# A graph network's attention layer: its prologue cut into three spans of nodes

## The reference, cut to what matters

```python
h = jnp.maximum(_layernorm(x, axis=-1), 0.0)
x = x + _L3_gnn_ref(h, src, dst, L3_gnn_qTrans, L3_gnn_kTrans, L3_gnn_vTrans)
...
q = (rowEmb @ qTrans).reshape(-1, HEADS, head_dim)
k = (colEmb @ kTrans).reshape(-1, HEADS, head_dim)
v = (colEmb @ vTrans).reshape(-1, HEADS, head_dim)
att = jnp.clip(jnp.einsum('ehd,ehd->eh', q, k), -10.0, 10.0)
expAtt = jnp.exp(att)
attNorm = jax.ops.segment_sum(expAtt, rows, num_segments=n_nodes)[rows]
att = expAtt / (attNorm + 1e-08)
res = (att[:, :, None] * v).reshape(-1, EMB)
out = jax.ops.segment_sum(res, rows, num_segments=n_nodes)
```

## Time and profile before

| | us |
|---|---|
| median of 3 runs | 2742.87 (2740.80 to 2744.53) |
| the profiled execution | 2741.29 |
| its span, first to last instruction | 2739.6 |
| DVE busy in it | 1842.0 (67%) |
| POOL busy | 1266.8 (46%) |
| PE busy | 1204.0 (44%) |
| ACT busy | 783.7 (29%) |

### The profile page before, as it was taken

One profiled execution on the slowest core, in us unless ns is written; L12 is line 12 of the kernel. 1 busy time (PEld: TensorE's weight loads), 2 busy tenths in 40 slices (PEclk: granted clock), 3 DMA queues, 4 the chain that ended last, 5 costly groups with the idle time before them and its releaser, 6 DMA issues. The chain is left out here.

```text
span 2739.6 us, 40317 instructions
## 1 busy us (share of the span) xinstructions
PE 1204.0 (44%) x12203; PEld 596.2 (22%) x12203; DVE 1842.0 (67%) x3710; ACT 783.7 (29%) x1927; POOL 1266.8 (46%) x973
## 2 busy tenths in 40 slices
PE   1111111111111111111110169978799629998898
PEld 1111111111111111111110023333343413333334
DVE  9988788888888888888885101111201539999997
ACT  0000000133332223121111300000000229999996
POOL 2788888888888888888888000000000000100001
PEclk6555555555555555555555589999899859999997
DMA  6776776689888889775666998889579282333231
GB/s 222 240 220 191 222 221 182 141 216 222 202 218 217 206 210 221 161 156 125 135 148 130 283 421 355 350 361 416 217 286 366 76 132 84 88 88 88 85 87 48
DMA packets 506207, 550.60 MB, mean 201 GB/s; under 512 B 129536, under 2 KB 452669, under 8 KB 504381
## 3 DMA queue, kind: packets, MB, share of 16 engines
q1 hardware_dynamic: 137773, 303.52, 30.9%
q10 hardware_dynamic: 255792, 245.78, 27.9%
q0 software_dynamic: 112608, 0.85, 9.7%
HBM read 381.75 MB, written 168.31 MB: 201 GB/s over the span
## 5 line engine op out<-in xcount | busy, mean ns | idle before, releaser
L610 POOL DMA_INDIRECT table<-amount,cell x782 | 1210.6, 1548 | 295.8 <-issue 281.1
L431 DVE SCALAR_TENSOR_TENSOR equal<-key_row,keys,masks 128x1280 bf16<-128x1280 f32 (+9 forms) x790 | 692.2, 943 | 0.2 <-DVE parts L417 0.2
L563 PE MATMUL totals<-parts_g,equal 128*128 128x6 bf16 x4345 | 129.0, 167 | 1022.8 <-DVE is_tile L440 1022.6
L283 ACT ACTIVATE w_tile<-cells 128x128 f32<-128x128 f32 x600 | 179.2, 301 | 779.4 <-issue 769.3
L563 PEld LDWEIGHTS totals<-parts_g,equal 128*128 128x128 bf16 x4345 | 122.2, 104 | 1034.3 <-DVE is_tile L440 1034.0
L944 PE MATMUL banks<-tiles,xs_pair 128*64 128x512 f32 (+1 forms) x1512 | 316.5, 567 | 5.8 <-DMA tiles<-counts_dram 5.0
L1257 POOL MEMSET o_t<- 128x64 f32 x1 | 0.2, 151 | 650.6 <-POOLq L719 650.6
L1267 POOL COPY v_tile<-v_all 128x128 f32 x175 | 51.6, 296 | 506.1 <-PE banks_d L1320 432.8
L423 DVE SCALAR_TENSOR_TENSOR equal_tail<-key_row,keys,masks 128x1280 bf16<-128x1280 f32 x156 | 235.2, 1546 | 20.1 <-issue 17.1
L1305 PE MATMUL banks_d<-q,k 96*128 (+2 forms) x700 | 194.5, 368 | 80.3 <-DMA k<-parts_dram 47.1
L1152 ACT ACTIVATE att<-banks_d,shift 128x1024 f32<-128x1024 f32 (+1 forms) x175 | 199.2, 1138 | 76.4 <-PE banks_d L1305 76.0
(11 more groups left out here) (226 smaller groups left out, 1513.0 us busy)
## 6 DMA issues: line engine op xcount, KB each, us to landing
table<-zeros ACTq DMA_DIRECT2D x100, 800.0 KB
cells<-table ACTq DMA_DIRECT2D x24, 3200.0 KB
key_row<-keys_dram SPq DMA_DIRECT2D x79, 640.0 KB
tiles<-counts_dram SPq DMA_DIRECT2D x27, 1664.0 KB, 10.0
tiles<-weights_dram SPq DMA_DIRECT2D x27, 1664.0 KB, 9.5
tiles<-counts_dram SPq DMA_DIRECT2D x27, 1536.0 KB, 8.7
tiles<-weights_dram SPq DMA_DIRECT2D x27, 1536.0 KB, 8.3
weights_dram<-w_tile ACTq DMA_DIRECT2D x24, 1600.0 KB
```

The source lines that it names most:

```text
L283: ins = nc.scalar.activation(w_tile[:, b, s], cells[:, s, :, 0], ACT.Copy, accum_out=deg_parts[:, s, bass.ds(t, 1)])
L431: ins = nc.vector.scalar_tensor_tensor(equal[b][:, OWN_AT[j]:OWN_AT[j + 1]], key_row[:, b, j * P:GE], keys[:, bass.ds(g * G + j, 1)], own_ ...
L563: nc.tensor.matmul(sums, equal[b][:, at:at + P], parts_g[:, b, j, :], start=False, stop=True, skip_group_check=True)
L610: nc.gpsimd.indirect_dma_start(out=table, out_offset=bass.IndirectOffsetOnAxis(ap=cell[:, b, j:j + 1], axis=0), in_=amount[:, b, j, :], in ...
```

## The change

The prologue is cut in three spans of columns, `SPANS`: chunks 0 and 1 (1024 columns, 8 tiles), chunks 2 and 3 (1024), and chunks 4 to 6 (1152). PE mixes its transposes and projections chunk by chunk; ACT alone does all 14 copies; DVE splits span by span. `parts_dram` now has the layout of `q6` and `k6`: head, block, feature. SP stores for each span twelve pieces of 64 rows, one for each of the six blocks of q and of k, so a part that stands in three blocks is stored three times. It then reloads each span with two DMAs of 96 rows and 4 heads. PE waits for the first span before the first score; the other two waits stand at tiles 8 and 16 of the first chunk, whose steps are written out instead of looped.

```diff
-    parts_dram = nc.dram_tensor("parts_dram", [3, 2, HEADS, HD, NR], BF16, kind="Internal").ap()
+    parts_dram = nc.dram_tensor("parts_dram", [2, HEADS, NPART, HD, NR], BF16, kind="Internal").ap()
+    SPANS = [(0, 2), (2, 4), (4, len(CHUNKS))]
+    span_cols = [slice(CHUNKS[a][0], sum(CHUNKS[b - 1])) for a, b in SPANS]
...
-            keep(0)
-            keep(1)
-            place(0)
-            keep(2)
-            place(1)
-            place(2)
+            def keep(span):
+                for part_no in range(3):
+                    sp.wait_ge(parts_ready, 3 * span + part_no + 1)
+                    for side, part_of in ((0, QPART), (1, KPART)):
+                        for n in range(NPART):
+                            if part_of[n] == part_no:
+                                sp.dma_start(parts_dram[side, :, n, :, span_cols[span]],
+                                             part[side * D:(side + 1) * D, part_no, span_cols[span]]
+                                             ).then_inc(parts_stored[span], 16)
+
+            def place(span):
+                sp.wait_ge(parts_stored[span], 16 * 2 * NPART)
+                for side, to in ((0, q6), (1, k6)):
+                    sp.dma_start(to[:, :, span_cols[span]],
+                                 parts_dram[side, :, :, :, span_cols[span]].rearrange("h n d c -> (n d) h c")
+                                 ).then_inc(rows_placed[span], 16)
+
+            for span in range(3):
+                keep(span)
+                place(span)
             blocks = counts_dram.rearrange("(s p) d -> p s d", p=P)
...
+            copy_h(0)
+            for n in range(len(CHUNKS)):
+                if n + 1 < len(CHUNKS):
+                    copy_h(n + 1)
+                copy_qk(n)
...
-            for n in range(3):
-                nc.vector.tensor_copy(part[:, n], qk_t[:]).then_inc(parts_ready, 1)
-                dve.wait_ge(parts_ready, n + 1)
-                if n < 2:
-                    link(nc.vector.tensor_tensor(qk_t[:], qk_t[:], part[:, n], ALU.subtract))
+            for span, (_, last) in enumerate(SPANS):
+                dve.wait_ge(qk_copied, last)
+                rest = qk_t[:, span_cols[span]]
+                for n in range(3):
+                    piece = part[:, n, span_cols[span]]
+                    nc.vector.tensor_copy(piece, rest).then_inc(parts_ready, 1)
+                    dve.wait_ge(parts_ready, 3 * span + n + 1)
+                    if n < 2:
+                        link(nc.vector.tensor_tensor(rest, rest, piece, ALU.subtract))
...
+            turn_chunk(0)
+            turn_chunk(1)
             for n, (c0, w) in enumerate(CHUNKS):
-                pe.wait_ge(h_t_ready[n % 2], n // 2 + 1)
+                pe.wait_ge(h_t_ready, n + 1)
                 nc.tensor.matmul(banks[:, n, 0:w], k["qk"][:], h_t[:, c0:c0 + w], start=True, stop=True
                                  ).then_inc(qk_ready, 1)
-            for e in range(2):
-                pe.wait_ge(qk_copied[e], 1)
+                if n + 2 < len(CHUNKS):
+                    turn_chunk(n + 2)
+            pe.wait_ge(qk_copied, len(CHUNKS))
...
-            pe.wait_ge(rows_placed, 16 * 2 * NPART)
+            pe.wait_ge(rows_placed[0], 32)
...
+                    if first:
+                        for t in range(2, T):
+                            for span in (1, 2):
+                                if t * P == span_cols[span].start:
+                                    pe.wait_ge(rows_placed[span], 32)
+                            step(t, t % RING, t // RING)
+                        return
...
-            with pe.Fori(0, SC - 1) as ci:
+            chunk(0, 4, 4, first=True)
+            with pe.Fori(1, SC - 1) as ci:
                 chunk(ci, 4, 4)
```

More of the change, by code:

```diff
@@ L1042, in attention_layer @@
     h_ready, turned = sem("h_ready_d"), sem("turned_d")
-    h_t_ready, qk_copied = [sem(f"h_t_ready{e}") for e in range(2)], [sem(f"qk_copied{e}") for e in range(2)]
+    h_t_ready, qk_copied = sem("h_t_ready"), sem("qk_copied")
     qk_ready, parts_ready, v_cleared = sem("qk_ready"), sem("qk_parts_ready"), sem("v_cleared")
     parts_stored = [sem(f"parts_stored{n}") for n in range(3)]
-    rows_placed = sem("rows_placed")
+    rows_placed = [sem(f"rows_placed{n}") for n in range(3)]
     v_made, v_copied = sem("v_made"), sem("v_copied")
@@ L1068, in over_tiles @@
                 body(RING * i + j, j, c_reg * USES + i, c_reg * T + RING * i + j)
[L1070 to L1078, removed]
     N_SCORED = -(-N // 64) * 64
@@ L1139, in _, with copy_h, copy_qk @@
             nc.scalar.activation(stat[:, 2], stat[:, 1], ACT.Sqrt).then_inc(std_ready, 1)
-            copy_banks(act, nc.scalar.copy, 0)
+            def copy_h(n):
+                act.wait_ge(turned, n + 1)
+                c0, w = CHUNKS[n]
+                nc.scalar.copy(h_t[:, c0:c0 + w], banks[0:D, n, 0:w]).then_inc(h_t_ready, 1)
+            def copy_qk(n):
+                act.wait_ge(qk_ready, n + 1)
+                c0, w = CHUNKS[n]
+                nc.scalar.copy(qk_t[:, c0:c0 + w], banks[:, n, 0:w]).then_inc(qk_copied, 1)
+            copy_h(0)
[3 more added lines that the diff above has]
+                copy_qk(n)
             act.wait_ge(consts_set, 2)
@@ L1177, in _ @@
             nc.vector.memset(shift[:, 1:2], -CLIP).then_inc(consts_set, 1)
-            copy_banks(dve, nc.vector.tensor_copy, 1)
-            for e in range(2):
-                dve.wait_ge(qk_copied[e], 1)
-            for n in range(3):
-                nc.vector.tensor_copy(part[:, n], qk_t[:]).then_inc(parts_ready, 1)
-                dve.wait_ge(parts_ready, n + 1)
-                if n < 2:
-                    link(nc.vector.tensor_tensor(qk_t[:], qk_t[:], part[:, n], ALU.subtract))
+            for span, (_, last) in enumerate(SPANS):
[7 more added lines that the diff above has]
+                        link(nc.vector.tensor_tensor(rest, rest, piece, ALU.subtract))
             dve.wait_ge(v_made, 1)
@@ L1275, in _, with turn_chunk @@
             pe.wait_ge(h_ready, 1)
-            for c0, w in CHUNKS:
+            def turn_chunk(n):
+                c0, w = CHUNKS[n]
                 for t in range(c0 // P, (c0 + w) // P):
@@ L1291, in _, with steps @@
             pe.wait_ge(consts_set, 2)
-            pe.wait_ge(rows_placed, 16 * 2 * NPART)
+            pe.wait_ge(rows_placed[0], 32)
             pe.sem_inc(counts_turned, RING)
             pe.sem_inc(values_added, RING)
-            def steps(ci, width):
+            def steps(ci, width, first=False):
                 W = columns(width)
@@ L1345, in steps, with chunk @@
                 return scores_of, tiles, values_of
-            def chunk(ci, width, next_width):
-                scores_of, tiles, values_of = steps(ci, width)
+            def chunk(ci, width, next_width, first=False):
+                scores_of, tiles, values_of = steps(ci, width, first)
                 tiles()
```

## The result

| | us |
|---|---|
| before, median of 6 | 2742.59 |
| changed kernel, median of 6 | 2759.48 (2755.57 to 2766.86) |
| ratio | 1.0066, 95% interval 1.0053 to 1.0079 |
| forecast | 2784 (2747 to 2808), slower 0.78 |

The direction was right and the time is in the range, but the slowdown is 17 us where 42 were forecast. The rival "four engines that don't meet" (2753) came nearer.

What follows compares the result with a forecast made beforehand. It took the loop's start, held by stores, reloads and the first counts, to shift the end, ACT and DVE being full. Counts at 2283.2 against 2240.98 gave +42: 2783.5, stated as 2784 us, range 2747 to 2808.

Steps and rivals of the forecast that it cites:

- four engines that don't meet: Rival on the prologue's stores: 1.26 and 1.42 us each, +11 us, 2753; chance 0.27.
- first span stored: Prologue, span 0: 2.5 us fixed plus twelve stores at 2.1 us after the first part, stored at 2205.3.
- The order: SP's queue: first load of counts comes behind `place(2)`, so the loop still starts behind all three spans.
- Four engines: Prologue stores: destination's outermost size 4 gives each store four DMA engines at most; share 0.25.
- sixteen: Rival on the stores: rows dealt over 16 engines, 0.3 us a store, 21 us earlier, 2722; chance 0.16.
- The price of one store: 64-row store on four partly meeting engines: 2.1 us (2.36 for 1152 columns), between 1.26 free and 2.5 halved.
- The lower bound: Best price of a 64-row store: four engines at 26 GB/s each, 104 GB/s together, 1.26 us.
- The full price for four engines: Port rule, engines 0 and 2, 1 and 3 meeting in every store: stores 94 us instead of 79, end 15 us later.
- The first part: Prologue's first split: first part ready at 2177.6 instead of 2184.60, 7 us gained; a 512-column projection costed at 0.90 us.
- The reload: Two 96-row reloads per span at 300 GB/s: 5.2 us, 5.9 for the third span.
- the fixed part: Time from a DMA's issue to its landing beyond the transfer itself, taken as 2.5 us.
- The cover: Prologue: split, ACT's 14 copies (8 us) and PE's v matmuls (8.03 us) stay hidden if stores take longer than DVE.

Runs made afterwards that it cites:

- e3: Changed kernel with SP's queue reordered: first loads of counts issued between the spans instead of behind the third reload; 2742.13 us, 0.9990 of before.
- e8: e1 with loads of counts between the spans as in e3, dealt out otherwise (tiles 0-4, 5-6, 7-12); 2705.11 us, 0.9862 of before.
- e1: Changed kernel with the 64 rows ordered feature, head, so a store's destination is one block and sixteen engines store; 2727.74 us, 0.9949 of before.
- e2: Changed kernel with every store read from partitions 32 to 95, so no two of four engines read 32 apart (traffic only); 2758.99 us, 1.0052 of before.
- e7: Changed kernel with one span of 3200 columns instead of three, and rows ordered feature, head for sixteen engines; 2742.41 us, 1.0000 of before.

## Why the prediction was wrong in size

By its own steps, against the profile after. Each duration runs from one event to the next, on SP's queue except for the first and the last (PE's transposes).

| step | forecast | measured | difference |
|---|---|---|---|
| first transpose to first part | 5.9 | 8.3 | +2.4 |
| first span stored | 27.7 | 21.3 | -6.4 |
| reload and second span | 32.9 | 23.4 | -9.5 |
| reload and third span | 36.0 | 25.8 | -10.2 |
| third reload and counts | 9.0 | 10.3 | +1.3 |
| sum | 111.5 | 89.1 | -22.4 |

- **The order** was right: the load of counts stands behind the third reload, and the loop with it. PE's first scores came 38.6 us after the first transpose (41.3 forecast) and changed nothing. e3 and e8 show it by taking it away.
- **Four engines** was right: share 0.26, and e1 shows what it costs. The 53-row store was enough to rule sixteen out. The rule of the Trainium skill ("DMA: Bandwidth & Descriptors", Why a DMA increments its semaphore by 16 and not by 1), the largest number up to 16 that divides the outermost size on both sides, gives the 4 that is seen.
- **The price of one store** is the term that was mis-sized: 2.1 us taken, 1.27 measured (131,072 bytes at 103 GB/s). The lower bound was the right end, and with it the sum says +11. The trace has +19.8: the other 9 us are 2.4 for the first part, 3.7 in the stores of the first span (21.3, where the cheap store gives 17.6) and 3 in the later steps. I put the value near halves, because readers might meet. They do when they are many: sixteen engines on 64 partitions get 205 GB/s (e1), four engines lose 3 us in the first span (e2), and nothing after. That a meeting costs by how full the shared path is would fit both, four engines asking for a quarter of the 416 GB/s of sixteen; it is my reading, and no run tried other numbers of engines.
- The rule of the Trainium skill ("SBUF — State Buffer", Door 1: The DMA port swizzle) by which partitions 32 apart share a port agrees with e1's 205 GB/s and with e2's first span. The full price for four engines that the prediction made of it (94 us of stores) does not come out: the trace shows 102 to 103 GB/s in spans two and three.
- **The first part** came 2.4 us later than worked out. The timeline shows a projection at 2.07 us where the row gave 0.90:

```profile
2175.07 2.07 PE L1296 MATMUL banks_d<-h_t_d,qk 64*128 64x512 f32 x2
...
2180.79 0.69 DVE L1191 CAST qk_part<-qk_t 128x1024 bf16<-128x1024 f32 x1 [7.17 <-ACT qk_t L1142]
```

Two such projections stand before the first part, 2.3 us of the 2.4. The windows, of before and then of after (in the last columns the granted clock, DMA share, GB/s):

```profile
2176.00:2182.00 6.00, 6.00 (x20) 2.84 (x17) 2.19 (x5) 2.56 (x5) 0.00 (x0) 1.00 0.00 0
...
2180.00:2200.00 20.00, 19.59 (x60) 12.09 (x60) 14.06 (x15) 6.47 (x12) 0.00 (x0) 0.50 0.22 72
```

The granted clock is 0.50 after, the lower of PE's two levels (1.2 GHz), and 1.00 before (2.4 GHz), where PE had begun at 0.50 as well and rose some 4 us after its first transpose. Waits are not what the trace shows for it: from 2173.23 to 2192 PE has no idle time in the rows of after either. What differs is the mix, all 25 transposes ahead of the projections before, four and one in turn after. Whether that kept the level low stays open; no run tried it alone. The duration was taken from rows at the higher level, and the change did not keep it.
- **The reload** at 263 GB/s (300 taken) and **the fixed part** of 2.5 us were near enough: together under 2 us a span.
- **The cover** held: DVE's split, ACT's fourteen copies and PE's v matmuls (10.92 us at the lower clock, where they were 8.03) ended before the first span had landed. It held because the stores were slow: in e1 and e8 the first scores wait for the copy of v (2.21 us).

## What to carry to other kernels

Before a DMA is reshaped, look at the outermost size that its instruction will carry on either side: the destination here fell apart in 4 blocks and was stored by 4 engines, and reordering rows upstream (the columns of a weight, two small copies) gave all 16 back. Where a wait is made earlier, look at what the next instruction on that engine waits for, and at what stands on the queue ahead of it: here both had to go, and each alone gave a part. And a price from one row holds for that row's surroundings: the shared price came from sixteen engines on 16 partitions, and four engines on 64 did not pay it; the projection's price came from a stretch at the higher clock. What a slow transfer hides comes to light when it is made fast, as the copy of v in e8.

## What the runs showed of the hardware

- Sixteen engines that store from 64 partitions move 205 GB/s busy at 0.93 (e1) and 228 busy at 1.01 (e7), from 128 partitions 416; four engines from 64 partitions move 103, which is four at full rate. A busy share near 1 does not say that the bytes move at full speed.
- Twelve issues of a 64-row store took SP 7.55 us in e1 and 7.79 in the first span of e2, and 13.50 in that of the changed kernel, which stores through four engines as e2 does. So the number of engines is not by itself what slows the issues; what does was not tried alone. Five loads of counts took 7.76 us behind a reload (e3). An instruction that waits for no semaphore can still hold a queue.
- PE was busy for 19.59 of 20 us in the changed prologue and the granted clock stayed at 0.50; before, in the same work in another order, it was 1.00 from some 4 us after the first transpose on.
- Six runs of the changed kernel lie 11 us apart and six of the one before 4, but in the two larger sets of 13 runs the one before lies 8 and 10 us apart. Differences of 3 us have to be read from the stretches of a trace, not from medians.
